# Wide attention layers: the weighted sum directly behind the scores, the turns last, and evacuations in that order

## The reference, cut to what matters

```python
q, k, v = x @ Wq, context @ Wk, context @ Wv           # 128 -> 16 heads x 64
dots = einsum('bhnd,bhmd->bhnm', q, k) * 64 ** -0.5     # 256 x 256 for each head
dots = dots - mask penalty                              # by query rows, or by keys
attn = softmax(dots, axis=-1)
out = einsum('bhnm,bhmd->bhnd', attn, v)
x = x + out.reshape(b, n, 1024) @ Wout
```

## Time and profile before

| | |
|---|---|
| median of three runs | 1729.38 us |
| the profiled execution's span | 1726.7 us |
| TensorE busy | 1472.2 us, 85% of the span |
| VectorE, ScalarE, GpSimd busy | 1094.5, 892.7, 705.5 us |
| first wide layer, first to last scores | 247.3 to 564.8 us |
| second wide layer | same code, between about 1240 and 1580 us |

### The profile page before, as it was taken

The page is one execution under the profiler, slowest core; times in us unless marked ns, Lnnn a source line. Parts: engine busy times, 40 slices in busy tenths (PEclk is TensorE's granted clock), DMA queues, the critical chain, the costliest instruction groups (busy, mean ns, idle before and its releaser), DMA issues.

```text
span 1726.7 us, 28570 instructions
## 1 busy us (share of the span) xinstructions
PE 1472.2 (85%) x9445; PEld 923.3 (53%) x9457; DVE 1094.5 (63%) x2396; ACT 892.7 (52%) x1947; POOL 705.5 (41%) x1039
## 2 busy tenths in 40 slices
PE   5787689999999577777867887699899999996898
PEld 1444346666666456666744444444466666665343
DVE  4544437777777699999954552533477777776444
ACT  1444346666666377777724444233366666663222
POOL 5443115444444489889843331100154444442000
PEclk9999699999999889999989999699999999998999
DMA  1006100000000000000000000000000000000000
GB/s 59 16 13 221 55 3 4 4 3 3 3 3 4 1 1 1 1 0 0 1 7 7 7 7 2 25 0 0 3 4 4 3 3 3 3 0 1 0 12 12
DMA packets 13669, 21.73 MB, mean 13 GB/s; under 512 B 3200, under 2 KB 10256, under 8 KB 13072
## 3 DMA queue, kind: packets, MB, share of 16 engines
q1 hardware_dynamic: 13584, 20.63, 3.4%
HBM read 19.58 MB, written 1.05 MB: 12 GB/s over the span
## 4 chain that ended last, share of the span: by engine, by line
PE 52%; DVE 25%; ACT 9%; issue 7%; POOL 5%; DVEq 0%; ACTq 0%; DMA 0%; SPq 0%; POOLq 0%
DVE sb_VP L649 6%; ACT sb_both L969 5%; PE bank L909 5%; PE bank L887 5%; PE bank L872 4%; DVE sb_both L1742 4%; PE bank L384 3%; DVE bank L1049 3%; POOL sb_QT L733 3%; PE bank L1781 3%; PE bank L860 3%; PE bank L1961 3%; PE bank L839 3%; DVE sb_wneg L1051 2%; PE bank L390 2%
## 5 line engine op out<-in xcount | busy, mean ns | idle before, releaser
L1117 POOL TENSOR_TENSOR sb_both<-sb_both,sb_winv 128x512 f32<-128x512 f32 x256 | 260.8, 1040 | 362.3 <-DVE sb_winv L1056 362.3
L1669 POOL TENSOR_TENSOR sb_KM<-sb_OT 128x1024 f32<-128x1024 f32 x128 | 240.1, 1912 | 31.4 <-DVE sb_both L1742 27.4
L969 ACT ACTIVATE sb_both<-bank,sb_wneg 128x256 f32<-128x256 f32 x512 | 235.1, 475 | 29.1 <-DVE sb_wneg L1051 28.8
L1573 PE MATMUL bank<-sb_ident,sb_both 128*128 128x128 f32 x1024 | 141.6, 288 | 60.1 <-DVE sb_both L1742 37.7
L649 DVE TENSOR_REDUCE sb_VP<-bank 128x8 f32<-128x2048 f32 (+1 forms) x64 | 111.1, 1758 | 94.8 <-PE bank L390 94.8
L1742 DVE SCALAR_TENSOR_TENSOR sb_both<-sb_KM,sb_best,bank 128x1024 f32<-128x1024 f32 x128 | 158.5, 1274 | 10.2 <-ACT bank L1644 10.2
L1573 PEld LDWEIGHTS bank<-sb_ident,sb_both 128*128 128x128 f32 x1024 | 120.2, 148 | 75.5 <-DVE sb_both L1742 49.2
L1051 DVE TENSOR_REDUCE sb_wneg<-bank 128x4 f32<-128x1024 f32 x128 | 156.8, 1225 | 4.4
L909 PE MATMUL bank<-sb_QT,sb_VP 128*64 128x256 f32 x1024 | 138.8, 392 | 19.0 <-DVE sb_QT L1063 13.3
L872 PE MATMUL bank<-sb_KM 64*128 64x256 f32 x1024 | 145.2, 402 | 4.9 <-ACT sb_both L969 4.9
L1644 ACT ACTIVATE bank<-sb_KM 128x1024 f32<-128x1024 f32 x128 | 129.8, 1024 | 36.0 <-DVE sb_both L1742 32.2
(11 more groups left out here) (257 smaller groups left out, 2760.4 us busy)
## 6 DMA issues: line engine op xcount, KB each, us to landing
sb_ctxT_in<-in_ctxT SPq DMA_DIRECT2D x32, 128.0 KB, 2.3
sb_F<-in_F SPq DMA_DIRECT2D x2, 1024.0 KB
sb_XO<-in_ctx SPq DMA_DIRECT2D x8, 128.0 KB, 2.0
sb_WQ<-in_WQ SPq DMA_DIRECT2D x2, 512.0 KB, 5.8
sb_WK<-in_WK SPq DMA_DIRECT2D x2, 512.0 KB, 6.8
sb_WV<-in_WV SPq DMA_DIRECT2D x2, 512.0 KB, 7.6
sb_WO<-in_WO SPq DMA_DIRECT2D x2, 512.0 KB, 8.5
sb_WKQ<-in_WKQ SPq DMA_DIRECT2D x1, 1024.0 KB, 9.1
```

Source lines behind the costliest of these rows:

```text
L969: last = act.activation(PRW[:, t % 4, h, i, :], s[:, h, i, :], ACT.Exp, bias=wneg[:, t % 4, h, i:i + 1], accum_out=wsum[:, t % 4, h, i:i + 1])
L1117: pool.tensor_tensor(p, p, winv[:, t % 4, :, i:i + 1].broadcast_to([P, 2, SEQ]), ALU.mult).then_inc(w_norm, 1)
L1573: last = pe.matmul(weight_bank(c), gated[:, h % 4, c * P:(c + 1) * P], ident[:], is_transpose=True, start=(h == 0 and c % 4 == 0), stop=(h ...
L1669: pool.tensor_tensor(dst, s[:, h, 0, :].unsqueeze(2).broadcast_to([P, NK, NK]), s[:, h, 1, :].unsqueeze(1).broadcast_to([P, NK, NK]), ALU. ...
```

## The change

On TensorE, `weighted` moves from behind `queries_keys` to directly behind `scores`, ahead of the output product, and `transposes` moves to the end of the step, behind `values` and `norm`. On ScalarE, `heads_out` moves ahead of the copy of the query and key product. On VectorE, the copy of the turned probabilities moves behind the copies of the values, of the turned x and of the context. No instruction is added or taken away, and no semaphore's counts change.

```diff
@@ wide_tensor, step
                 scores(b, t)
+                if behind or t >= 3:
+                    weighted(*back_by(b, t, 3))
                 if t == 3 and behind:
                     out_product(b - 1, PAIRS * b + 1)
                 if t < 6:
                     queries_keys(b, t + 2)
                 elif more:
                     queries_keys(b + 1, t - 6)
-                if behind or t >= 3:
-                    weighted(*back_by(b, t, 3))
-                if behind or t >= 2:
-                    transposes(*back_by(b, t, 2))
                 weighted_so_far = PAIRS * b + t - 2 if behind or t >= 3 else None
                 if t == 0:
                     values(b, 1, weighted_so_far)
...
                 if t == 7 and more:
                     values(b + 1, 0, weighted_so_far)
+                if behind or t >= 2:
+                    transposes(*back_by(b, t, 2))
@@ wide_scalar, step
+                if behind or t >= 3:
+                    heads_out(*back_by(b, t, 3))
                 if t < 6:
                     queries_keys(b, t + 2)
                 elif more:
                     queries_keys(b + 1, t - 6)
-                if behind or t >= 3:
-                    heads_out(*back_by(b, t, 3))
                 if behind or t >= 2:
                     copy_pt(*back_by(b, t, 2))
                 exps(b, t)
@@ wide_vector, step
                 if t == 3 and behind:
                     add_out(b - 1)
-                if behind or t >= 2:
-                    copy_pt(*back_by(b, t, 2))
                 if t == 0:
                     values(b, 1)
...
                 if t == 7 and more:
                     values(b + 1, 0)
+                if behind or t >= 2:
+                    copy_pt(*back_by(b, t, 2))
```

## The result

The changed kernel takes 1776.58 us, the median of four runs, against 1730.11 of the kernel before in the same runs: a ratio of 1.0268, 95% interval 1.0249 to 1.0287. It is slower by 46.5 us; forecast were 40, and 1769.4 us. The profiled execution has a span of 1776.4 us, 49.7 more than that of before; it is one execution, which took 1.6 us more than the median.

What follows compares the result with a forecast made beforehand. TensorE's own sequence was taken to bound the kernel; saved shape changes less new waits cost 20 us a layer, 40 for two, raising the span from 1726.7 to 1766.7, plus 2.7 for the median: 1769.4 us, range 1754 to 1786.

Steps and rivals of the forecast that it cites:

- The waits: TensorE's weighted sum waits for VectorE's copies in steps 3, 5, 7, 0 and 1: 4.70 us a batch.
- The chain from the exponentials over VectorE to the weighted sum: Earliest weighted sum: 5.20 us after the exponentials two steps earlier, plus VectorE's work ahead of its turns' copy, up to 2.09.
- the loop's head: Loop of ScalarE and VectorE, 4.66 us a step: from the inverse of the sums to the next mask addition, 0.10 us.
- The change of array shape: TensorE makes three changes of array shape a step instead of four: 0.15 us saved a step, bounds 0.1 to 0.35.
- the change from rows to columns: TensorE, scores to weighted sum: not in the trace, taken to cost like other changes; if free, saving about 0.3 us.
- The other edits: ScalarE's reordered copies, VectorE's moved turn copy, the next context's DMA and GpSimd's multiplication: priced at nothing.
- the first batch: Start of each layer, without an output product and with weighted sums from step 3 only: loses about 1.3 us.
- the falling clock: Rival: new waits lower TensorE's clock, one step a batch at 1.2 GHz, 56 us more, 1825 us; chance 0.05.
- the prediction's own list: Signs of being wrong: batch under 41.2 us, no wait ahead of the weighted sum, granted clock under 1.00 inside wide layers.
- six batches of each layer: Batches repeating the steady pattern, each 44.02 us against 41.18, 2.84 more: 17.0 us a layer.
- last batches: End of each layer, with no next batch to prepare: loses about 1.6 us.

Runs made afterwards that it cites:

- statistics behind: Changed kernel with VectorE's statistics and normalisation moved behind the step's copies, its turns' copy again ahead of the values' copy: 1754.7 us, ratio 1.0149.
- ScalarE's copies: Changed kernel with ScalarE making both copies of the turned probabilities and VectorE none: 1744.3 us, ratio 1.0078.
- together, with the turns ahead of the values: Changed kernel with turns ahead of values, VectorE's statistics and normalisation at the step's end, and both turn copies on ScalarE: 1712.6 us, ratio 0.9889.
- the run with the old order: Changed kernel with VectorE's order of before, the turns' copy ahead of the values' copy: 1779.8 us, ratio 1.0273.
- only the turns last: Changed kernel with TensorE's weighted sum back behind the query and key product, and ScalarE and VectorE in their order of before: 1779.7 us, ratio 1.0281.

## Why the prediction was right

*The waits.* Forecast in steps 3, 5, 7, 0 and 1 were 0.73, 1.28, 0.73, 0.39 and 1.57 us, measured 0.80, 1.27, 0.74, 0.49 and 1.66, and none in steps 2, 4 and 6. The chain from the exponentials over VectorE to the weighted sum is right in every link but the loop's head. The runs that shorten it (statistics behind, ScalarE's copies) win what was expected of them, and together, with the turns ahead of the values, they leave TensorE as the bound but for one wait of 0.34 us a batch.

*The change of array shape.* A plain step without a wait (step 6, 366.66 to 370.67) takes 4.01 us, against 4.16 in the earlier trace rows: 0.15 saved, as chosen. The scores' distance to the weighted sum is 1.06, the same as it was to the query product, so the change from rows to columns costs there what the one from rows to the full array costs; were it free, the saving would have been near 0.3. Behind the product of the full array the turns lost their slow entry, as foretold (1.04 us instead of 1.09). The Trainium skill ("TensorEngine Tiling (Array Packing)", Key Properties) says that going to another tiling mode drains the engine. These numbers fit that; that a drain is what is paid, no run shows.

*The other edits.* VectorE's moved copy costs 0.16 us a batch at most, as the run with the old order shows. ScalarE's exchange was not tried alone.

*The term that was too small* is the first batch: 1.3 us a layer in the sum, 4.0 measured (36.22 to 40.23, 36.23 to 40.28). The 2.6 us of low clock, which the sum put at nothing, make up the difference; they leave 1.4 for the waits. The prediction had the falling clock as a rival, with one step in every batch and 56 us as its price, and gave it 0.05 because the 1.49 us wait of the earlier trace rows left the clock up. The clock fell, but once a layer, where the new order puts a second wait right behind that one; by the prediction's own list, a granted clock under 1.00 inside a wide layer was a sign of being wrong. The waits of up to 1.66 us within the batches did not lower it: it was 1.00 from 267.69 to 589.00. The Trainium skill ("TensorE: Matmul & The Clock Gate", "Why this matters for your kernels") warns of idle gaps between bursts. It speaks of single gaps, not of two close together, as they stand here.

The profiled difference of 49.7 us adds up so: first batches 8.1 (forecast 2.6), six batches of each layer 18.8 and 17.4 (forecast 17.0 each), last batches to their last scores 2.9 (3.2), and 2.5 in the stretches between and behind, whose code, from the last weighted sums on, the change does not touch and whose time varies by several us from kernel to kernel (675.3 to 682.3 between the layers) and between two profiles of the changed kernel.

That the measured time lies in the stated range is in part luck. The range was made for errors in the waits and in the change of shape, and these came out 0.26 us a batch above the forecast and as chosen. The low clock, about 5.2 of the 7.2 us by which the forecast missed, was not in it.

## What to carry to other kernels

A consumer moved to the front of a step gives up slack that its inputs may need: before moving it, add up the chain from the last thing that the old order finished early (here the turns) to the copy that the consumer waits for, over all engines and all that stands ahead on each queue. The early weighted sum that lost 2.7% here was part of a version that won 1.1% once the turns came earlier again and the copy it waited for no longer stood behind the longest work of VectorE. And a steady state worked out well says little of the first pass, where waits stand closer together.

## What the runs showed of the hardware

The clock: with waits of 1.49 and 2.06 us and one group of scores between them, the granted clock fell to 0.50 during the second, for 6.8 us, in both layers of all five profiles that have these waits. In the old order's first batch, with 0.95, 1.49 and 1.00 and more work between them, it stayed at 1.00; with only the turns last, a fourth wait of 1.04 us comes behind these three, and it fell for 3.4 us in both layers. Behind the last scores of a layer, waits of 1.39 and 2.46 us were followed by 3.4 us of low clock, by 13.7, or by none (the granted clock was 1.00 from 589.13 to 611.00 in the changed kernel), so the waits alone do not say when it falls.

VectorE's normalisation (two instructions) is slower where GpSimd adds the bias at the same time, which only the first wide layer does: 0.81 us against 0.60. GpSimd and VectorE of the changed kernel in the first layer, then VectorE in the second:

```profile
405.39 0.73 POOL L1125 TENSOR_TENSOR sb_x<-sb_x,sb_bo 128x256 f32 x1
```

```profile
405.64 0.81 DVE L1017 TENSOR_SCALAR sb_xn<-sb_x,sb_mv,sb_rstd 128x128 f32 x2
...
1425.33 0.60 DVE L1017 TENSOR_SCALAR sb_xn<-sb_x,sb_mv,sb_rstd 128x128 f32 x2
```

Step 5 waits 0.21 us less in the second layer, whose batch is 0.23 shorter. The runs with the statistics behind show that it is the overlap: there the normalisation comes after GpSimd's addition, still in the first layer, and takes 0.60 (GpSimd, then VectorE, of the changed kernel with that edit).

```profile
397.77 0.73 POOL L1125 TENSOR_TENSOR sb_x<-sb_x,sb_bo 128x256 f32 x1
```

```profile
399.22 0.60 DVE L1017 TENSOR_SCALAR sb_xn<-sb_x,sb_mv,sb_rstd 128x128 f32 x2
```

Its batches are equally long in both layers (42.32 us). GpSimd's addition takes 0.73 us either way.
